# A graph layer's 8192 x 8192 adjacency product, streamed in loads of 8 MB through two ring slots instead of 4.5 MB through four

## The chip, the core and the metric

The kernel runs on one core of a Trainium2 chip. The metric is the device time of one execution in microseconds (us). The kernel before took 643.39 us, the median of 3 runs (643.38 to 643.44).

## What is computed

```python
agg = adj @ (x @ W_agg)                       # adj 8192 x 8192, x 8192 x 64, float32
y   = w[:, None] * relu(agg) + (1.0 - w)[:, None] * x
out = layernorm(x + y)                        # over the 64 columns of a row, eps 1e-5
```

`adj` is nearly all zeros but is given dense, 268.4 MB in float32.

## The kernel before

The host hands `adj` over transposed and cut into blocks, so that every load is contiguous in DRAM; this is not in the metric. The 64 row tiles of 128 rows are done in groups: `G` = 6 main groups of nine (`MAIN_SLOTS`), one mid group of nine (`MID_SLOTS`), and one last row tile. For a group the contraction runs over 64 k-tiles of 128. A main load (L128, L132) brings eight k-tiles (`SUB`) for nine row tiles: 128 partitions with one row of 8 x 9 x 128 x 4 = 36,864 bytes each, 4608 KB. `C` = 8 loads make a group. They go round a ring of four slots (`RING`). SP issues all of them on one DMA queue. Before each it waits on `slot_free`, which PE raises when it has used up the load that was in that slot (L127, L131, L135).

PE computes the transposed aggregate with `x` as the stationary operand (`contract`, L182 to L190). The array's 128 columns are used as two halves of 64. The halves take k-tiles of even and odd number, so the two halves of a bank hold partial sums, in three banks of 384 columns. `turn_back` (L192 to L201) then multiplies by `W_agg`, stacked twice in `wagg2`, which turns the sum round to rows and adds the halves. Before it ACT copies the banks to `aggT` (L257). Every product in the code is two records in the trace: 8 x 3 x 2 = 48 in all for a load, of 384 columns each. DVE does relu, residual and normalisation (L304 to L314, L292 to L302) beside the next group's loads.

The mid group is loaded in the same way, its last two loads in pieces of 4, 4 and 2, 2, 2, 2 k-tiles (`MID_TAIL`, L139 to L144), so that PE is soon done after the last. Then SP issues the store of the first 54 row tiles (L146), waits for slot 0 (L148), and issues ten loads of the last row tile into it (L150 to L153, `LAST_LOADS`). PE works these off (L222 to L229), the last two k-tiles against a ready `x @ W_agg` (L233 to L235), and the last rows are normalised and stored from ACT's queue (L269). The mid rows' store follows on SP's queue (L156).

Of the kernel before, what the change touches and what calls it, by code (L numbers as in the profile page):

```python
# [17 lines left out]
def gnn_residual_layernorm(nc, x, adj_main, adj_mid, adj_last, w, w_agg, out):  # L18
# [21 lines left out]
    BANKS = 3  # L40
    CHUNK = COLS // BANKS
    PER_BANK = MAIN_SLOTS // BANKS
# [4 lines left out]
    assert DIRECT_J0 % 2 == 0 and all(sum(pieces) == SUB for pieces in MID_TAIL) and MID_SLOTS == MAIN_SLOTS  # L47
# [11 lines left out]
    with ctx:  # L59
# [8 lines left out]

        ring = sb("ring", [P, RING, SUB * COLS])
        x_sb = sb("x_sb", [P, T, D])  # L70
# [5 lines left out]
        wagg2 = sb("wagg2", [P, D])  # L76
        ident = sb("ident", [P, P])
        eps = sb("eps", [P, 1])
        aggT = sb("aggT", [P, COLS])
# [13 lines left out]
        acc = bank[:, 0:BANKS]  # L93
        last_acc = bank[:, 3]
        last_rows = bank[:, 4, 0:D]

        xT_ps = bank[:, 3, 0:PAIRS * P]
        xw_ps = [bank[:, 4 + h, 0:PAIRS * D].rearrange("p (n d) -> p n d", d=D) for h in range(2)]
        rows_ps = bank[:, 5:5 + BANKS, 0:PER_BANK * D]

# [4 lines left out]
        x_in, w_in, wagg_in = sem("x_in"), sem("w_in"), sem("wagg_in")  # L105
        ident_zero, ident_ready = sem("ident_zero"), sem("ident_ready")
# [3 lines left out]
        last_done = sem("last_done")  # L110
# [9 lines left out]
        @block.sync  # L120
        def _(sp):
            sp.dma_start(x_sb[:], x.rearrange("(p t) d -> p t d", p=P)).then_inc(x_in, 16)  # L122
            sp.dma_start(w_sb[:], w.rearrange("(p t) -> p t", p=P)).then_inc(w_in, 16)  # L123
            for c in range(C):
                if c >= RING:

                    sp.wait_ge(slot_free, c - RING + 1)  # L127
                sp.dma_start(ring[:, c % RING], adj_main[0, c].rearrange("q s n -> q (s n)")).then_inc(loaded[c % RING], 16)  # L128
            with sp.Fori(1, G) as g:
                for c in range(C):  # L130
                    sp.wait_ge(slot_free, g * C + (c - RING + 1))  # L131
                    sp.dma_start(ring[:, c % RING],  # L132
                                 adj_main[bass.ds(g, 1), c].rearrange("o q s n -> (o q) (s n)")).then_inc(loaded[c % RING], 16)
            for c in range(C):
                sp.wait_ge(slot_free, MID * C + c - RING + 1)  # L135
                if c < WHOLE:
                    sp.dma_start(ring[:, c % RING], adj_mid[c].rearrange("q s n -> q (s n)")).then_inc(loaded[c % RING], 16)
                else:
                    s = 0  # L139
                    for k, n in enumerate(MID_TAIL[c - WHOLE]):  # L140
                        sp.dma_start(ring[:, c % RING, s * COLS:(s + n) * COLS],
                                     adj_mid[c, :, s:s + n].rearrange("q s n -> q (s n)")
                                     ).then_inc(mid_tail_loaded[c - WHOLE][k], 16)
# [12 lines left out]
            sp.dma_start(out_rows[:, MID_T0:LAST_T0], res[:, MID_T0:LAST_T0]).then_inc(stored, 16)  # L156

        @block.gpsimd
        def _(pool):
            nc.gpsimd.memset(ident[:], 0.0).then_inc(ident_zero, 1)  # L160
            pool.wait_ge(ident_zero, 1)
            nc.gpsimd.affine_select(out=ident[:], in_=ident[:], compare_op=ALU.not_equal, fill=1.0, base=0,
                                    pattern=[[-1, P]], channel_multiplier=1).then_inc(ident_ready, 1)
            nc.gpsimd.memset(eps[:], EPS).then_inc(eps_ready, 1)

        @block.tensor
        def _(pe):
# [14 lines left out]
            def contract(slot, j0, s0, n):  # L182
                for s in range(s0, s0 + n, 2):
                    for b in range(BANKS):
                        for h in range(2):
                            j = j0 + s + h
                            at = (s + h) * COLS + b * CHUNK
                            last = nc.tensor.matmul(acc[h * D:(h + 1) * D, b, 0:CHUNK], x_sb[:, j], ring[:, slot, at:at + CHUNK],  # L188
                                                    start=j < 2, stop=j >= T - 2)
                return last  # L190

            def turn_back(g):  # L192

                pe.wait_ge(dve_step, g * DVE_GROUP + DVE_PRE)
                for b in range(BANKS):
                    pe.wait_ge(agg_copied, g * BANKS + (b + 1))
                    for i in range(PER_BANK):
                        at = (b * PER_BANK + i) * P
                        last = nc.tensor.matmul(rows_ps[:, b, i * D:(i + 1) * D], aggT[:, at:at + P], wagg2[:],  # L199
                                                start=True, stop=True)  # L200
                    last.then_inc(rows_done, 1)  # L201

            with pe.Fori(0, G) as g:
                for c in range(C):
                    pe.wait_ge(loaded[c % RING], g * (16 * C // RING) + arrivals(c))
                    contract(c % RING, c * SUB, 0, SUB).then_inc(slot_free, 1)
                turn_back(g)
            for c in range(WHOLE):
                pe.wait_ge(loaded[c % RING], arrivals(MID * C + c))
                contract(c % RING, c * SUB, 0, SUB).then_inc(slot_free, 1)  # L210
            for i, pieces in enumerate(MID_TAIL):
                c = WHOLE + i
                s = 0
                for k, n in enumerate(pieces):
                    pe.wait_ge(mid_tail_loaded[i][k], 16)
                    last = contract(c % RING, c * SUB, s, n)
                    s += n
                last.then_inc(slot_free, 1)

            j = 0  # L220
            turn_back(MID)
            for k, n in enumerate(LAST_LOADS[:-1]):  # L222
                pe.wait_ge(last_loaded[k], 16)
                for s in range(n):
                    h = (j + s) % 2
                    last = nc.tensor.matmul(last_acc[h * D:(h + 1) * D, 0:P], x_sb[:, j + s],  # L226
                                            ring[:, 0, (j + s) * P:(j + s + 1) * P],
                                            start=j + s < 2, stop=j + s >= DIRECT_J0 - 2)
                j += n  # L229
# [3 lines left out]
            for j in range(DIRECT_J0, T):  # L233
                nc.tensor.matmul(last_rows, ring[:, 0, j * P:(j + 1) * P], xw[:, (j - DIRECT_J0) // 2, (j - DIRECT_J0) % 2],  # L234
                                 start=j == DIRECT_J0, stop=False)  # L235

            pe.wait_ge(agg_copied, LAST * BANKS + 1)
# [3 lines left out]
        def _(act):  # L241
            for h in range(2):
                act.dma_start(wagg2[h * D:(h + 1) * D, :], w_agg).then_inc(wagg_in, 16)

# [9 lines left out]
            def group(g):  # L254
                act.wait_ge(slot_free, g * C + C)
                for b in range(BANKS):
                    nc.scalar.copy(aggT[:, b * CHUNK:(b + 1) * CHUNK], acc[:, b, 0:CHUNK]).then_inc(agg_copied, 1)  # L257
                std_of(std[:], varsum[:], 1.0 / D, g * DVE_GROUP + (DVE_PRE + VAR_STEP))

            with act.Fori(0, G) as g:  # L260
                group(g)

                act.wait_ge(out_ready, g + 1)
            group(MID)
# [9 lines left out]
        def _(dve):  # L274
# [29 lines left out]
            with dve.Fori(0, LAST) as g:  # L304
                base = g * DVE_GROUP + DVE_PRE
                for b in range(BANKS):
                    dve.wait_ge(rows_done, g * BANKS + (b + 1))
                    slots = bass.ds(g * MAIN_SLOTS + b * PER_BANK, PER_BANK)
                    last = nc.vector.scalar_tensor_tensor(out=y[:, b * PER_BANK:(b + 1) * PER_BANK],  # L309
                                                          in0=rows_ps[:, b].rearrange("p (n d) -> p n d", d=D),  # L310
                                                          scalar=0.0, in1=over_row(w_sb[:, slots]),
                                                          op0=ALU.max, op1=ALU.mult)
                step(last, base + 1)
                normalise(g, g * MAIN_SLOTS, MAIN_SLOTS, base)  # L314

            v, t = y_last[:], LAST_T0
            dve.wait_ge(rows_done, LAST * BANKS + 1)
# [40 lines left out]
```

## Time and profile before

| | us |
|---|---|
| median of 3 runs | 643.39 |
| the profiled execution, its own time | 643.17 |
| span of its instructions | 641.1 |
| PE busy (matmuls) | 509.9 (80%) |
| DVE busy | 47.1 (7%) |
| ACT busy | 12.9 (2%) |
| DMA queue q1, share of 16 engines | 99.1% |
| read from HBM / written | 270.60 MB / 2.10 MB |

The profile is of one execution on the chip. Outside the span lie 643.17 - 641.1 = 2.1 us. Engine names: PE is the matrix engine, PEld its weight loads, DVE and ACT the vector and scalar engines, SPq and ACTq the instruction queues that issue DMAs. A packet is one row of one partition, or the 4 bytes with which a DMA engine reports its part of a load; a packet is placed by its start.

### The profile page before, as it was taken

To read this page: it belongs to the slowest core of one execution; us is meant where nothing else is said; L and a number is where in the kernel's file an instruction comes from. 1 tells how busy PE (TensorE), PEld (TensorE's weight loads), DVE (VectorE), ACT (ScalarE), POOL (GpSimd) and SP (SyncE) were. 2 spreads that over 40 slices of the span, in tenths; PEclk is the share of its full clock that TensorE was granted. 3 is DMA by queue.
4 is the path that set the end of the run, shared out by engine and by line. 5 is a ranking of instruction groups with operands and counts; after the bars stand their busy time and mean duration, and the time that the engine had idled before them with its cause. 6 is when DMAs were issued, how large, how long until landed. Compare 5 with 4: busy or idle time off the path is not lost.

```text
span 641.1 us, 6455 instructions
## 1 busy us (share of the span) xinstructions
PE 509.9 (80%) x2949; PEld 222.1 (35%) x2949; DVE 47.1 (7%) x80; ACT 12.9 (2%) x32; POOL 0.7 (0%) x7
## 2 busy tenths in 40 slices
PE   0778888878697878797788888796979788878896
PEld 0233334323233323242333343232424234333335
DVE  3000002000003000030000030000300000300004
ACT  0000000000000000000000000000000000000000
POOL 0000000000000000000000000000000000000000
PEclk9989889889999988998898898999998889898999
DMA  9999999999999999999999999999999999999996
GB/s 363 435 440 437 415 435 440 435 416 437 442 432 419 437 439 435 414 442 439 430 419 442 439 428 421 442 439 423 426 442 437 426 426 442 436 423 427 424 421 261
DMA packets 10967, 272.81 MB, mean 426 GB/s; under 512 B 1616, under 2 KB 2000, under 8 KB 3024
## 3 DMA queue, kind: packets, MB, share of 16 engines
q1 hardware_dynamic: 10656, 272.63, 99.1%
q8 instruction: 7, 0.11, 0.1%
q10 hardware_dynamic: 304, 0.07, 0.0%
HBM read 270.60 MB, written 2.10 MB: 425 GB/s over the span
## 4 chain that ended last, share of the span: by engine, by line
DMA 77%; PE 20%; SPq 2%; issue 0%; DVE 0%; ACT 0%; DVEq 0%
DMA ring<-adj_main_dram 62%; PE bank L188 19%; DMA ring<-adj_mid_dram 11%; DMA ring<-adj_last_dram 4%; SPq L151 1%; PE bank L226 1%; PE bank L199 0%; SPq L128 0%; SPq L132 0%; PE bank L234 0%; ACT aggT L257 0%; SPq L123 0%; SPq L122 0%; DVE res L324 0%; ACT std_last L252 0%
## 5 line engine op out<-in xcount | busy, mean ns | idle before, releaser
L188 PE MATMUL bank<-ring,x_sb 128*64 128x384 f32 x2688 | 484.6, 521 | 112.2 <-DMA ring<-adj_main_dram 99.8
L188 PEld LDWEIGHTS bank<-ring,x_sb 128*64 128x64 f32 x2688 | 199.2, 146 | 393.8 <-issue 248.2
L309 DVE SCALAR_TENSOR_TENSOR y<-bank,w_sb 128x192 f32<-128x192 f32 x21 | 7.5, 358 | 571.7 <-PE bank L199 571.7
L257 ACT COPY aggT<-bank 128x384 f32<-128x384 f32 x21 | 8.7, 487 | 568.4 <-PE bank L188 568.4
L199 PE MATMUL bank<-wagg,aggT 128*128 128x64 f32 x126 | 15.5, 277 | 4.1 <-ACT aggT L257 4.1
L199 PEld LDWEIGHTS bank<-wagg,aggT 128*128 128x128 f32 x126 | 14.6, 192 | 8.8 <-ACT aggT L257 7.5
L226 PE MATMUL bank<-ring,x_sb 128*64 128x128 f32 x124 | 7.9, 278 | 1.6 <-DMA ring<-adj_last_dram 1.5
L226 PEld LDWEIGHTS bank<-ring,x_sb 128*64 128x64 f32 x124 | 6.8, 136 | 2.6 <-DMA ring<-adj_last_dram 2.4
L172 PE MATMUL bank<-ident,x_sb 128*128 128x128 f32 x1 | 0.4, 447 | 8.9 <-DMA x_sb<-x_dram 8.9
L294 DVE TENSOR_TENSOR y<-y,res 128x576 f32<-128x576 f32 x7 | 5.3, 758 | 1.0
L296 DVE SCALAR_TENSOR_TENSOR y<-rowsum,y 128x576 f32<-128x576 f32 x7 | 5.3, 759 | 0.2
L302 DVE TENSOR_TENSOR res<-y,rstd 128x576 f32 x7 | 5.3, 758 | 0.2
L298 DVE TENSOR_TENSOR sq<-y 128x576 f32<-128x576 f32 x7 | 5.3, 757 | 0.2
L299 DVE TENSOR_REDUCE varsum<-sq 128x9 f32<-128x576 f32 x7 | 5.3, 754 | 0.2
L295 DVE TENSOR_REDUCE rowsum<-y 128x9 f32<-128x576 f32 x7 | 5.3, 754 | 0.2
L290 DVE TENSOR_TENSOR res<-x_sb,two_minus_w 128x4096 f32<-128x4096 f32 x1 | 4.4, 4427 | 0.0
L172 PEld LDWEIGHTS bank<-ident,x_sb 128*128 128x128 f32 x1 | 0.2, 183 | 8.8 <-issue 8.8
L252 ACT ACTIVATE std<-varsum,eps 128x9 f32<-128x9 f32 x7 | 2.1, 303 | 42.9 <-DVE varsum L299 42.9
L301 DVE RECIPROCAL rstd<-std 128x9 f32<-128x9 f32 x7 | 1.5, 216 | 2.6 <-ACT std L252 2.6
L245 ACT ACT_TABLE_LOAD x1 | 1.3, 1283 | 2.0 <-issue 2.0
L284 DVE COPY xw<-bank 128x64 f32<-128x64 f32 x2 | 0.4, 220 | 10.5 <-PE bank L178 10.5
L178 PE MATMUL bank<-wagg,xT 64*128 64x64 f32 x4 | 0.7, 437 | 0.4 <-ACT xT L247 0.4
(22 smaller groups left out, 5.8 us busy)
## 6 DMA issues: line engine op xcount, KB each, us to landing
ring<-adj_main_dram SPq DMA_DIRECT2D x48, 4608.0 KB, 35.5
ring<-adj_mid_dram SPq DMA_DIRECT2D x6, 4608.0 KB, 34.8
ring<-adj_mid_dram SPq DMA_DIRECT2D x2, 2304.0 KB, 32.8
ring<-adj_mid_dram SPq DMA_DIRECT2D x4, 1152.0 KB, 29.5
x_sb<-x_dram SPq DMA_DIRECT2D x1, 2048.0 KB, 8.0
out_dram<-res SPq DMA_DIRECT2D x1, 1728.0 KB, 36.7
ring<-adj_last_dram SPq DMA_DIRECT2D x2, 768.0 KB, 32.5
ring<-adj_last_dram SPq DMA_DIRECT2D x1, 640.0 KB, 26.2
```

The lines of the kernel that those rows point to most:

```text
L151: sp.dma_start(ring[:, 0, j * P:(j + n) * P], adj_last[:, j:j + n].rearrange("q s n -> q (s n)")).then_inc(last_loaded[k], 16)
L188: last = nc.tensor.matmul(acc[h * D:(h + 1) * D, b, 0:CHUNK], x_sb[:, j], ring[:, slot, at:at + CHUNK], start=j < 2, stop=j >= T - 2)
L199: last = nc.tensor.matmul(rows_ps[:, b, i * D:(i + 1) * D], aggT[:, at:at + P], wagg2[:], start=True, stop=True)
L226: last = nc.tensor.matmul(last_acc[h * D:(h + 1) * D, 0:P], x_sb[:, j + s], ring[:, 0, (j + s) * P:(j + s + 1) * P], start=j + s < 2, stop ...
L257: nc.scalar.copy(aggT[:, b * CHUNK:(b + 1) * CHUNK], acc[:, b, 0:CHUNK]).then_inc(agg_copied, 1)
L294: step(nc.vector.tensor_tensor(v, v, residual, ALU.add), base + 2)
L295: step(nc.vector.tensor_reduce(rowsum[:, 0:n], v, AX.X, ALU.add), base + 3)
L296: step(nc.vector.scalar_tensor_tensor(out=v, in0=over_row(rowsum[:, 0:n]), scalar=-1.0 / D, in1=v, op0=ALU.mult, op1=ALU.add), base + 4)
L298: step(nc.vector.tensor_tensor(s, v, v, ALU.mult), base + 5)
L299: step(nc.vector.tensor_reduce(varsum[:, 0:n], s, AX.X, ALU.add), base + VAR_STEP)
L302: nc.vector.tensor_tensor(residual, v, over_row(rstd[:, 0:n]), ALU.mult).then_inc(out_ready, 1)
L309: last = nc.vector.scalar_tensor_tensor(out=y[:, b * PER_BANK:(b + 1) * PER_BANK], in0=rows_ps[:, b].rearrange("p (n d) -> p n d", d=D), s ...
```

## The change

A load becomes sixteen k-tiles for eight row tiles: rows of 65,536 bytes, 8192 KB, four loads to a group. There are seven main groups of eight, a mid group of seven and the last row tile. The ring has two slots. The last row tile's loads have a buffer of their own (`last_sb`), and no wait before them. In a main group the column halves of the array take row tiles 0 to 3 and 4 to 7, with the same k-tile: one bank of 512 columns, two products (four records) to a k-tile, 64 records to a load. Turning back takes four products with a block diagonal `wagg_diag` (zeroed by POOL, filled by two DMAs on ACT's queue). The mid group keeps the halves by k-tile, in two banks of 448 columns; its rows are 57,344 bytes, its last two loads are cut into 8, 8 and 4, 4, 4, 2, 2. ACT makes one copy per group, DVE's relu step is two instructions in a main group and one in the mid group. Cut to its core:

```diff
-MAIN_SLOTS = 9
-MID_SLOTS = 9
+MAIN_SLOTS = 8
+MID_SLOTS = 7
-SUB = 8
-RING = 4
-MID_TAIL = ((4, 4), (2, 2, 2, 2))
+SUB = 16
+RING = 2
+MID_TAIL = ((8, 8), (4, 4, 4, 2, 2))
+        last_sb = sb("last_sb", [P, T * P])
+        wagg_diag = sb("wagg_diag", [P, P])
...
             sp.dma_start(out_rows[:, 0:MID_T0], res[:, 0:MID_T0]).then_inc(stored, 16)
-
-            sp.wait_ge(slot_free, LAST * C - RING + 1)
             j = 0
             for k, n in enumerate(LAST_LOADS):
-                sp.dma_start(ring[:, 0, j * P:(j + n) * P],
+                sp.dma_start(last_sb[:, j * P:(j + n) * P],
...
+            nc.gpsimd.memset(wagg_diag[:], 0.0).then_inc(diag_zero, 1)
...
+            def main_loads(g):
                 for c in range(C):
                     pe.wait_ge(loaded[c % RING], g * (16 * C // RING) + arrivals(c))
-                    contract(c % RING, c * SUB, 0, SUB).then_inc(slot_free, 1)
+                    for s in range(SUB):
+                        j = c * SUB + s
+                        for h in range(2):
+                            at = s * COLS + h * HALF * P
+                            last = nc.tensor.matmul(acc[h * D:(h + 1) * D, :], x_sb[:, j], ring[:, c % RING, at:at + HALF * P],
+                                                    start=j == 0, stop=j == T - 1)
+                    last.then_inc(slot_free, 1)
+
+            def turn_back(g):
+                pe.wait_ge(agg_copied, g + 1)
+
+                pe.wait_ge(dve_step, g * DVE_GROUP + DVE_PRE)
+                for k in range(HALF):
+                    last = nc.tensor.matmul(rows_ps[:, k * P:(k + 1) * P], aggT[:, k * P:(k + 1) * P], wagg_diag[:],
+                                            start=True, stop=True)
+                last.then_inc(rows_done, 1)
+
+            pe.wait_ge(diag_in, 32)
+            with pe.Fori(0, G) as g:
+                main_loads(g)
                 turn_back(g)
...
+            last.then_inc(mid_done, 1)
+            pe.wait_ge(agg_copied, G + 1)
+            for i in range(MID_SLOTS):
+                turned = nc.tensor.matmul(mid_rows[:, i * D:(i + 1) * D], aggT[:, i * P:(i + 1) * P], wagg2[:],
+                                          start=True, stop=True)
+            turned.then_inc(rows_done, 1)
...
+            act.wait_ge(diag_zero, 1)
+            for h in range(2):
+                act.dma_start(wagg_diag[h * D:(h + 1) * D, h * D:(h + 1) * D], w_agg).then_inc(diag_in, 16)
...
+                nc.scalar.copy(aggT[:, 0:HALF * P], acc).then_inc(agg_copied, 1)
...
+            nc.scalar.copy(aggT[:].rearrange("p (b n) -> p b n", b=MID_BANKS), mid_acc).then_inc(agg_copied, 1)
```

## Rows read from the trace of the kernel before

**Rows 1.** The page, 40 slices of 16 us: DMA engines' busy tenths, and GB/s.
```profile
DMA  9999999999999999999999999999999999999996
GB/s 363 435 440 437 415 435 440 435 416 437 442 432 419 437 439 435 414 442 439 430 419 442 439 428 421 442 439 423 426 442 437 426 426 442 436 423 427 424 421 261
```

**Rows 2.** The page, chain of work that ended last, by engine and by line.
```profile
DMA 77%; PE 20%; SPq 2%; issue 0%; DVE 0%; ACT 0%; DVEq 0%
DMA ring<-adj_main_dram 62%; PE bank L188 19%; DMA ring<-adj_mid_dram 11%; DMA ring<-adj_last_dram 4%; SPq L151 1%; PE bank L226 1%; PE bank L199 0%; SPq L128 0%; SPq L132 0%; PE bank L234 0%; ACT aggT L257 0%; SPq L123 0%; SPq L122 0%; DVE res L324 0%; ACT std_last L252 0%
```

**Rows 3.** Costliest groups: busy us, mean ns of one, idle before and its releaser.
```profile
L188 PE MATMUL bank<-ring,x_sb 128*64 128x384 f32 x2688 | 484.6, 521 | 112.2 <-DMA ring<-adj_main_dram 99.8
L296 DVE SCALAR_TENSOR_TENSOR y<-rowsum,y 128x576 f32<-128x576 f32 x7 | 5.3, 759 | 0.2
```

**Rows 4.** Issues on SP's queue: KB each, median us from issue to landing.
```profile
ring<-adj_main_dram SPq DMA_DIRECT2D x48, 4608.0 KB, 35.5
```

**Rows 5.** DMA of 97.45:446.83, 32 main loads: packets, then queue q1 (packets, MB, share).
```profile
DMA packets 4608, 150.98 MB, mean 432 GB/s; under 512 B 512, under 2 KB 512, under 8 KB 512
q1 hardware_dynamic: 4607, 150.96, 100.3%
```

**Rows 6.** DMA of 602:633: mid pieces, the store, the last row tile's loads.
```profile
DMA packets 1827, 12.96 MB, mean 418 GB/s; under 512 B 204, under 2 KB 238, under 8 KB 1031
```

**Rows 7.** By stretch: length, busy PE, PEld, DVE, ACT, POOL, granted clock, DMA share, GB/s.
```profile
152.04:160.00 7.96, 7.96 (x48) 3.36 (x48) 0.00 (x0) 0.00 (x0) 0.00 (x0) 1.00 1.03 445
173.85:183.50 9.65, 9.63 (x48) 3.90 (x48) 0.00 (x0) 0.00 (x0) 0.00 (x0) 0.82 0.99 428
315.80:325.97 10.17, 10.17 (x46) 4.16 (x48) 0.00 (x0) 0.00 (x0) 0.00 (x0) 0.71 1.03 442
```

**Rows 8.** The chain in order of time, its longest piece of PE: start, us, what.
```profile
315.80 10.90 PE bank L188 x48
```

**Rows 9.** PE in order of time: start, us, records, [idle before and its releaser].
```profile
97.45 2.80 PE L188 MATMUL bank<-ring,x_sb 128*64 128x384 f32 x16 [1.45 <-DMA ring<-adj_main_dram]
162.95 7.96 PE L188 MATMUL bank<-ring,x_sb 128*64 128x384 f32 x48 [2.95 <-DMA ring<-adj_main_dram]
173.87 9.65 PE L188 MATMUL bank<-ring,x_sb 128*64 128x384 f32 x48 [2.96 <-DMA ring<-adj_main_dram]
195.71 7.96 PE L188 MATMUL bank<-ring,x_sb 128*64 128x384 f32 x48 [0.16 <-DMA ring<-adj_main_dram]
630.96 5.33 PE L226 MATMUL bank<-ring,x_sb 128*64 128x128 f32 x84 [0.35 <-DMA ring<-adj_last_dram]
```

**Rows 10.** Packets of 96.75:97.00, then of 97.00:97.25, before the load used from 97.45.
```profile
DMA packets 5, 0.11 MB, mean 442 GB/s; under 512 B 2, under 2 KB 2, under 8 KB 2
DMA packets 1, 0.04 MB, mean 147 GB/s; under 512 B 0, under 2 KB 0, under 8 KB 0
```

**Rows 11.** The last store: its issue, and GB/s of 638.5:641.1 in 40 slices.
```profile
639.14 0.35 ACTq L269 DMA_DIRECT2D out_dram<-res  x1
GB/s 0 0 0 0 0 0 0 0 0 0 0 0 0 0 0 0 0 0 0 0 0 0 0 110 225 134 36 0 0 0 0 0 0 0 0 0 0 0 0 0
```

**Rows 12.** Around a group's end: start, us, what, [idle before].
```profile
105.45 1.24 ACT L257 COPY aggT<-bank 128x384 f32<-128x384 f32 x3 [95.84 <-PE bank L188]
105.98 2.22 PE L199 MATMUL bank<-wagg,aggT 128*128 128x64 f32 x18 [0.58 <-ACT aggT L257]
```

**Rows 13.** PE at the end of the mid group and in the last row tile.
```profile
621.80 2.16 PE L188 MATMUL bank<-ring,x_sb 128*64 128x384 f32 x12 [0.59 <-DMA ring<-adj_mid_dram]
624.62 2.19 PE L199 MATMUL bank<-wagg,aggT 128*128 128x64 f32 x18 [0.67 <-ACT aggT L257]
627.20 1.09 PE L226 MATMUL bank<-ring,x_sb 128*64 128x128 f32 x16 [0.38 <-DMA ring<-adj_last_dram]
632.54 3.50 PEld L226 LDWEIGHTS bank<-ring,x_sb 128*64 128x64 f32 x60 [0.30 <-DMA ring<-adj_last_dram]
```

More of the change, by code:

```diff
@@ L46, in gnn_residual_layernorm @@
     assert C * SUB == T == sum(LAST_LOADS) and LAST_T0 + LAST_SLOTS == T and C % RING == 0
-    assert DIRECT_J0 % 2 == 0 and all(sum(pieces) == SUB for pieces in MID_TAIL) and MID_SLOTS == MAIN_SLOTS
+    assert DIRECT_J0 % 2 == 0 and all(sum(pieces) == SUB for pieces in MID_TAIL) and HALF * P == 512
     DVE_PRE = 2
@@ L92, in gnn_residual_layernorm @@
         bank = psum("bank", [P, 8, 512])
-        acc = bank[:, 0:BANKS]
+        acc = bank[:, 0]
+        mid_acc = bank[:, 1:1 + MID_BANKS, 0:MID_CHUNK]
         last_acc = bank[:, 3]
         last_rows = bank[:, 4, 0:D]
+        rows_ps = bank[:, 5]
+        mid_rows = bank[:, 6, 0:MID_SLOTS * D]
         xT_ps = bank[:, 3, 0:PAIRS * P]
-        xw_ps = [bank[:, 4 + h, 0:PAIRS * D].rearrange("p (n d) -> p n d", d=D) for h in range(2)]
-        rows_ps = bank[:, 5:5 + BANKS, 0:PER_BANK * D]
+        xw_ps = [bank[:, 6 + h, 0:PAIRS * D].rearrange("p (n d) -> p n d", d=D) for h in range(2)]
         loaded = [sem(f"loaded{r}") for r in range(RING)]
@@ L180, in _ @@
             last.then_inc(xw_done, 1)
[L182 to L201, printed above, removed]
@@ new lines, in mid_contract @@
+            def mid_contract(c, s0, n):
+                for s in range(s0, s0 + n, 2):
+                    for b in range(MID_BANKS):
+                        for h in range(2):
+                            j = c * SUB + s + h
+                            at = (s + h) * MID_COLS + b * MID_CHUNK
+                            last = nc.tensor.matmul(mid_acc[h * D:(h + 1) * D, b], x_sb[:, j],
+                                                    ring[:, c % RING, at:at + MID_CHUNK], start=j < 2, stop=j >= T - 2)
+                return last
@@ L215, in _ @@
                     pe.wait_ge(mid_tail_loaded[i][k], 16)
-                    last = contract(c % RING, c * SUB, s, n)
+                    last = mid_contract(WHOLE + i, s, n)
                     s += n
-                last.then_inc(slot_free, 1)
+            last.then_inc(mid_done, 1)
[4 more added lines that the diff above has]
+            turned.then_inc(rows_done, 1)
             j = 0
-            turn_back(MID)
             for k, n in enumerate(LAST_LOADS[:-1]):
@@ L243, in _ @@
                 act.dma_start(wagg2[h * D:(h + 1) * D, :], w_agg).then_inc(wagg_in, 16)
+            act.wait_ge(diag_zero, 1)
+            for h in range(2):
+                act.dma_start(wagg_diag[h * D:(h + 1) * D, h * D:(h + 1) * D], w_agg).then_inc(diag_in, 16)
             nc.scalar.preload_act_table_set("sqrt_and_others")
@@ L252, in std_of @@
                 nc.scalar.activation(out_std, var, ACT.Sqrt, bias=eps[:, 0:1], scale=scale).then_inc(std_ready, 1)
-            def group(g):
+            with act.Fori(0, G) as g:
                 act.wait_ge(slot_free, g * C + C)
-                for b in range(BANKS):
-                    nc.scalar.copy(aggT[:, b * CHUNK:(b + 1) * CHUNK], acc[:, b, 0:CHUNK]).then_inc(agg_copied, 1)
+                nc.scalar.copy(aggT[:, 0:HALF * P], acc).then_inc(agg_copied, 1)
                 std_of(std[:], varsum[:], 1.0 / D, g * DVE_GROUP + (DVE_PRE + VAR_STEP))
-            with act.Fori(0, G) as g:
-                group(g)
                 act.wait_ge(out_ready, g + 1)
-            group(MID)
+            act.wait_ge(mid_done, 1)
+            nc.scalar.copy(aggT[:].rearrange("p (b n) -> p b n", b=MID_BANKS), mid_acc).then_inc(agg_copied, 1)
+            std_of(std[:, 0:MID_SLOTS], varsum[:, 0:MID_SLOTS], 1.0 / D, MID * DVE_GROUP + DVE_PRE + VAR_STEP)
             act.wait_ge(last_done, 1)
@@ L302, in normalise @@
                 nc.vector.tensor_tensor(residual, v, over_row(rstd[:, 0:n]), ALU.mult).then_inc(out_ready, 1)
-            with dve.Fori(0, LAST) as g:
+            with dve.Fori(0, G) as g:
                 base = g * DVE_GROUP + DVE_PRE
[L306 to L312, printed above, removed]
+                dve.wait_ge(rows_done, g + 1)
+                for h in range(2):
+                    last = nc.vector.scalar_tensor_tensor(
+                        out=y[:, h * HALF:(h + 1) * HALF],
+                        in0=rows_ps.rearrange("p (k h d) -> p h k d", h=2, d=D)[:, h], scalar=0.0,
+                        in1=over_row(w_sb[:, bass.ds(g * MAIN_SLOTS + h * HALF, HALF)]), op0=ALU.max, op1=ALU.mult)
                 step(last, base + 1)
                 normalise(g, g * MAIN_SLOTS, MAIN_SLOTS, base)
+            base = MID * DVE_GROUP + DVE_PRE
+            dve.wait_ge(rows_done, G + 1)
+            step(nc.vector.scalar_tensor_tensor(out=y[:, 0:MID_SLOTS], in0=mid_rows.rearrange("p (n d) -> p n d", d=D),
+                                                scalar=0.0, in1=over_row(w_sb[:, MID_T0:LAST_T0]),
+                                                op0=ALU.max, op1=ALU.mult), base + 1)
+            normalise(MID, MID_T0, MID_SLOTS, base)
             v, t = y_last[:], LAST_T0
-            dve.wait_ge(rows_done, LAST * BANKS + 1)
+            dve.wait_ge(rows_done, LAST + 1)
             step(nc.vector.tensor_scalar(v, last_rows, 0.0, w_sb[:, t:t + 1], ALU.max, ALU.mult), LAST_STEP0 + 1)
```

30 lines of the change are left out of this document (15 added, 15 removed).

## Prediction

> **What bounds the kernel now.** I read the slices first. The DMA engines are at nine tenths or more in every slice but the last, at 414 to 442 GB/s, save the first, which holds the start [rows 1]. The chain of waits says the same: 77% of it is DMA, and the 20% that it gives to PE are PE working on a load while the queue behind it is full [rows 2]. PE waits for loads 112 us in all [rows 3]. A main load takes 35.5 us from issue to landing though its data need a quarter of that: 32 loads took 349.38 us, 10.92 us each [rows 4, 5]. So some three loads always stand in the queue, and the q1 share is 100.3% [rows 5]. Nothing that PE, ACT or DVE save counts; only bytes, packets, or a queue that runs dry can move the time.
>
> **Price of a packet.** Two stretches with full engines but different rows. In the first (349.38 us, 16 engines: 5590 engine-us) 4608 packets carry 150.98 MB; in the second (31 us, 496 engine-us) 1827 packets carry 12.96 MB [rows 5, 6]. With a time per byte and a time per packet, two equations give 27.26 GB/s per engine and 11.3 ns per packet. The second stretch's MB are rounded, and it holds stores as well; 0.04 MB is 1.5 us of engine time, so I take 10 ns, with 5 and 13 as bounds. Below it could be nothing, if the lower rate of the second stretch (418 against 432 GB/s) is not the packets' doing.
>
> **Packets saved.** Per engine a load is 8 rows and one report, 9 packets. Before: 54 whole loads and 6 pieces, 60 x 9 = 540. After: 7 x 4 = 28 main, 2 whole mid loads and 7 pieces, 37 x 9 = 333. Saved: 207 x 10 ns = 2.1 us (1.0 to 2.7). The last row tile's ten loads are as before, as are the bytes of `adj`, `x` and the output.
> The Trainium skill (DMA: Bandwidth & Descriptors, section Why small descriptors are slow) puts a packet's fixed cost at about 3 cycles, and the section Where 436 GB/s comes from puts the cycle at 850 MHz: by that estimate 3.5 ns, and the saving 0.7 us, 642.7 us in all. The two stretches disagree with it here by a factor of three.
>
> **Added.** Two small loads for `wagg_diag`, 4 rows of 256 bytes and a report on each engine, twice: 10 packets, about 0.15 us with their bytes, on full engines, so they count. POOL's extra memset and ACT's wait come before `x` has landed, and PE's wait for `diag_in` is long over when the first 8 MB land, at about 28 us. Sum: 2.1 - 0.15, some 1.9 us less.
>
> **Two slots.** This is the step that could cost. By the rates above a load now takes 8 x (2404 + 10) + 10 ns = 19.3 us. PE's records follow each other at 7.96 / 48 = 166 ns for 384 columns and 5.33 / 84 = 63 ns for 128 [rows 9]: 0.40 ns per column, so 217 ns for 512, or 221 in proportion. 64 records: 14.0 us. Before, a slot was refilled three loads ahead; now the refill is issued when PE is done, with one load left in the queue. Measured from the slowest engine's last byte of load c: PE starts 0.45 to 0.7 us later (last two reports in 96.75:97.00, PE at 97.45 [rows 9, 10]), works 14.0 us, SP issues, and the first packet starts 0.85 us after the issue (639.14, first bytes in the slice from 640.0 [rows 11]; nearest row, a small store, I take 0.9). That is 0.6 + 14.0 + 0.9 = 15.5 us against 19.3: 3.8 us to spare at the higher clock.
> The clock takes some of it. PE works at the granted clock 1.00 (2.4 GHz) in one load and at 0.82 or 0.71 in others, which mixes 2.4 and 1.2 GHz [rows 7]; of two loads before which PE had idled 2.95 and 2.96 us, one ran at the higher level throughout and one did not [rows 7, 9]. Idle time grows to 19.3 - 14.0 = 5.3 us, so I expect most loads to begin at 1.2 GHz. The worst load before took 10.90 instead of 7.96 us [rows 8, 9], 2.9 us more. If that is a stretch of fixed length: 14.0 + 2.9 = 16.9, and 18.4 us with the rest, 0.9 us to spare. If it grew with the load (14.0 x 10.90 / 7.96 = 19.2 us) the queue would run dry by 1.4 us. I take the first, since the higher clock returned inside each load, and since a longer busy time shortens the next idle one. I cost the two slots at nothing; the cover is the 0.9 us.
>
> **Turning back.** Before: 0.5 us of copy, 2.2 us for 18 records, and PE is still back in time, with 0.16 us idle [rows 9, 12]. After: one copy of 512 columns, about 0.6 us, and 8 records of 128 columns at 123 to 170 ns, 1.4 us at most. After a slow last load PE is back at 16.9 + 2.0 = 18.9 us, before the next load; and `slot_free` has been raised before it, so the refill does not wait for it. DVE's work is seven or eight instructions of under 0.76 us [rows 3], beside a group of 77 us; ACT's is one copy. Neither is waited for.
>
> **The end.** The store before the last loads grows by 2 row tiles and the mid store shrinks by 2. The queue order is the same. Before, PE took up the last mid piece at 621.80, and the first last load reached it at 627.20, 5.4 us later, after 0.38 us idle [rows 13]. After: 2 k-tiles x 4 records x 193 ns = 1.5 us, one copy of 896 columns (0.9 us), 14 records (1.7 us): 4.2 us, still hidden. From 632.54 PE's pace sets the end, 60 records and the last products [rows 13]: unchanged. The wait for slot 0 that goes was hidden by a full queue. So the DMA saving passes through whole.
>
> **Sum.** 643.17 - 1.9 = 641.2 for a profiled execution, whose span would be 639.2; its own time stood 0.2 below the median, so the median comes out at 641.5 us. A measurement of this kernel can tell about 0.2%, 1.3 us, from no change.
>
> **Rivals.**
> 1. No gain: a 64 KB row is moved as two packets, or the packet price is far under 10 ns. Split rows make 28 x 17 + 2 x 9 + 63 = 557 packets against 540: with `wagg_diag` 0.3 us more, 643.7. Nothing in the trace moved more than 36,864 bytes in one packet, so the profile can't exclude it. A price of 3 or 4 ns gives 642.7. Chance 0.17, at 643.5.
> 2. Slower, the queue runs dry. It decides at a PE time of 19.3 - 0.6 - 0.9 = 17.8 us per load; beyond it each us costs a us on each load. Where the low clock lasts in proportion, 1.4 us on each of the 30 whole loads is 42 us; on every third load it is 14 us: 643.4 - 1.9 + 14 = 655.5. For it: idle grows from 2.96 to 5.3 us, and the start of a transfer is known only from a small store. Against it: the worst load of 56 had 2.9 us of loss. Chance 0.17.
> 3. Slower, the rate itself falls. In the new layout the partitions' rows lie 65,536 bytes apart in DRAM, and engines in step read at large powers of two from each other; before it was 36,864. The last loads already have a power of two, 32,768, and their stretch ran at 418 instead of 432 GB/s [rows 5, 6]. If that was the pitch and not the packets, the 235 MB of main loads at 418 take 18 us more: 661.6. Against it: the packet price explains the whole difference, and the pieces of the mid group in that stretch have no such pitch. Chance 0.06.
> The Trainium skill (DMA: Bandwidth & Descriptors, Latency and other measured facts) reports copies with rows 512 KiB apart at 207 GB/s, against 214 at full rate, and 103 at 4 MiB; by 3% it would be some 20 us here. No run yet shows a pitch of 64 KiB on this chip.
>
> **How the numbers follow.** The forecast, 641.5 us, has 0.60; its own range is 640.6 to 642.6 by the packet's bounds, and 0.04 of it lies within 0.2% of the time before (above 642.1). So faster 0.56, no change 0.04 + 0.17 = 0.21, slower 0.17 + 0.06 = 0.23. The range takes the forecast, the first rival and the mild end of the second (the queue dry by 0.3 us on ten loads): 640.3 to 646.0. What it leaves out is the larger part of rivals 2 and 3, under 0.2.
>
> **What would show it.** Right: in a stretch of whole main groups, 9 packets per engine per load, 433.5 GB/s or a little above, q1 share 100%; main loads landing every 19.3 us; issue to landing about 22 us (19.3 plus what is left of the load before it); PE idle 2 to 5 us before each, with low clock at many starts. Wrong: twice as many data packets (rival 1); SP's refills issued later than 17.8 us after a landing and a q1 share under 100% (rival 2); full engines at fewer GB/s (rival 3).

## The result and the profile after

The changed kernel takes 662.08 us (median of 4, 658.65 to 664.19) against 643.41 us beside it: 1.0285 of the time before, 95% interval 1.0266 to 1.0304. It is slower by 18.7 us where 1.9 us less was forecast. The profiled execution took 658.65 us with a span of 656.9.

The page after, DMA engines' busy tenths and GB/s in 40 slices of 16 us, to be held against [rows 1], and the chain of work that ended last, against [rows 2]:

```profile
DMA  9999999899999999999999999999999999999995
GB/s 389 447 383 436 443 388 431 371 423 447 443 387 447 383 439 447 391 435 395 447 447 443 427 407 447 439 391 447 443 427 379 411 447 447 399 416 422 394 395 213
...
q1 hardware_dynamic: 7344, 272.63, 97.7%
...
DMA 59%; PE 37%; SPq 3%; issue 0%; DVE 0%; ACT 0%; DVEq 0%
```

The bytes are the same, the packets fewer, and yet slices of 371 to 395 GB/s now stand between slices of 447. PE's share of the chain has gone from 20% to 37%: PE is what releases a load's slot, and the DMA queue now waits for that. q1's share of the engines has fallen from 99.1% to 97.7%. Even that understates it, as the next views show.

PE in order of time (start, us, records, idle before and its releaser), against [rows 9]; the starts are the landings of the loads:

```profile
28.39 16.68 PE L194 MATMUL bank<-ring,x_sb 128*64 128x512 f32 x64 [17.80 <-DMA ring<-adj_main_dram]
47.73 15.55 PE L194 MATMUL bank<-ring,x_sb 128*64 128x512 f32 x64 [2.66 <-DMA ring<-adj_main_dram]
69.28 16.72 PE L194 MATMUL bank<-ring,x_sb 128*64 128x512 f32 x64 [6.00 <-DMA ring<-adj_main_dram]
88.92 15.44 PE L194 MATMUL bank<-ring,x_sb 128*64 128x512 f32 x64 [2.93 <-DMA ring<-adj_main_dram]
...
208.76 16.95 PE L194 MATMUL bank<-ring,x_sb 128*64 128x512 f32 x64 [5.69 <-DMA ring<-adj_main_dram]
...
288.91 16.13 PE L194 MATMUL bank<-ring,x_sb 128*64 128x512 f32 x64 [5.67 <-DMA ring<-adj_main_dram]
308.25 13.95 PE L194 MATMUL bank<-ring,x_sb 128*64 128x512 f32 x64 [3.21 <-DMA ring<-adj_main_dram]
```

From 288.91 to 308.25 is 19.34 us, the forecast's length of a load; from 47.73 to 69.28 it is 21.55. From the second landing (47.73) to the last main one (563.02) there are 26 loads in 515.3 us; at 19.35 each they take 503.1. So 12.2 us are lost in the main groups. PE takes 13.95 us for a load at the full granted clock, and up to 16.95 where the clock is lower:

```profile
208.76:225.71 16.95, 16.95 (x64) 5.08 (x64) 0.00 (x0) 0.00 (x0) 0.00 (x0) 0.82 1.00 433
269.28:283.23 13.95, 13.95 (x64) 4.51 (x64) 4.65 (x8) 0.30 (x1) 0.00 (x0) 1.00 0.93 404
```

(By stretch, columns as in [rows 7].) Both lengths are the forecast's own, 14.0 and 16.9. What was not forecast is what happens in the queue. This is the refill of the slot that PE, at work from 28.39 on, has used up: its issue, then the packets of three stretches, those under 512 bytes being the engines' reports on the load in front of it (such short stretches show more than the real rate, since a packet counts whole where it starts):

```profile
45.11 0.33 SPq L133 DMA_DIRECT2D ring<-adj_main_dram  x1
```

```profile
DMA packets 27, 0.72 MB, mean 901 GB/s; under 512 B 16, under 2 KB 16, under 8 KB 16
DMA packets 3, 0.20 MB, mean 246 GB/s; under 512 B 0, under 2 KB 0, under 8 KB 0
DMA packets 2, 0.13 MB, mean 218 GB/s; under 512 B 0, under 2 KB 0, under 8 KB 0
```

They are 46.4:47.2, 47.2:48.0 and 48.4:49.0. All 16 engines have reported by 47.2, but only 11 have begun the new load by then, three more by 48.0, and the last two after 48.4, at 48.6 and 48.8, 3.5 and 3.6 us after the issue. These first rows took 2.5 to 3.4 us in the trace, where a row takes 2.42 us otherwise. An engine that has run empty starts late and slowly.

The plainest case is in run e8 below, where all 16 engines had been empty for 4.8 us when the refill was issued. The issue, and the packets of 52.88:54.8:

```profile
52.88 0.33 SPq L133 DMA_DIRECT2D ring<-adj_main_dram  x1
DMA packets 16, 1.05 MB, mean 546 GB/s; under 512 B 0, under 2 KB 0, under 8 KB 0
```

The first of the 16 rows starts at 53.84, 0.97 us after the issue, the last at 54.71, 1.8 us after it, and they take 2.8 to 3.3 us each.

I call the time from a refill's issue to the first engine's report on the load in front of it the lead: how much the engine that is furthest ahead still had to do. Of the 26 main refills after the second landing, read one by one in the trace, with the excess of the landing interval over 19.35 us:

| lead | refills | excess in all |
|---|---|---|
| under 2 us (four of them negative: issued after the first engine was empty) | 10 | 9.2 us |
| 2.0 to 2.9 us | 7 | 2.5 us |
| 3.1 us and over | 9 | 0.5 us |

The table goes by the first engine, while a load has landed only with the last, so it is no law for the single refill: the load behind a lead of -0.5 us (issue 127.13) took 19.3 us, because the engines that ran empty were those that were ahead; their reports came 2.7 us apart before it and 0.6 us after it.

Not all of this loss comes from the leads. In e2 below, where leads are 7.3 us and over, one interval is still 1.3 us too long (20.6 us, landing at 87.3). In it one packet of 16 KB passes on the queue that the page calls "instruction" (from 71.27, for 1.1 us). The row that starts right behind it, at 72.35, takes 2.89 us, and one engine is late from then on: the reports on a load come 1.8 us apart instead of 0.5. The queues of e2 in 70:76:

```profile
q1 hardware_dynamic: 37, 2.42, 93.8%
q8 instruction: 1, 0.02, 1.1%
```

The kernel before has such packets too; with one of them, at 36.6, its load that lands at 42.2 takes 12.0 us instead of 10.9. In the changed kernel two of them, at 52.53 and 92.78, fall into two of the four longest intervals, which the trace can't divide between the two causes.

The rest of the loss is in the mid group, whose loads are shorter still (16.9 us) and are issued behind PE's work on an 8-tile load (leads of 0.4 and 0.9 us for the second and the fourth). From the last main landing (563.02) to the last mid piece it takes 73.4 us; in e2 below, where PE is out of the way, it takes 68.2.

```profile
636.43 1.72 PE L218 MATMUL bank<-ring,x_sb 128*64 128x448 f32 x8 [0.51 <-DMA ring<-adj_mid_dram]
```

### The profile page after: what moved, and what is told of

It reads as the page before. It is cut to its first block, busy times and chain, and to the rows that moved or that the text cites. A ratio compares the mean times of both kernels' runs of the same rounds, so it can differ in the third digit from the quotient of the medians.

```text
span 656.9 us, 4963 instructions
## 1 busy us (share of the span) xinstructions
PE 506.4 (77%) x2253; PEld 171.2 (26%) x2253; DVE 46.5 (7%) x81; ACT 9.5 (1%) x20; POOL 0.9 (0%) x8
## 3 DMA queue, kind: packets, MB, share of 16 engines
q1 hardware_dynamic: 7344, 272.63, 97.7%
## 4 chain that ended last, share of the span: by engine, by line
DMA 59%; PE 37%; SPq 3%; issue 0%; DVE 0%; ACT 0%; DVEq 0%
DMA ring<-adj_main_dram 53%; PE bank L194 34%; DMA last_sb<-adj_last_dram 3%; DMA ring<-adj_mid_dram 3%; PE bank L218 2%; SPq L155 2%; SPq L147 0%; SPq L137 0%; PE bank L251 0%; SPq L152 0%; PE bank L243 0%; SPq L128 0%; SPq L133 0%; SPq L127 0%; DVE res L348 0%
## 5 line engine op out<-in xcount | busy, mean ns | idle before, releaser
L194 PE MATMUL bank<-ring,x_sb 128*64 128x512 f32 x1792 | 434.0, 646 | 122.5 <-DMA ring<-adj_main_dram 122.5
L194 PEld LDWEIGHTS bank<-ring,x_sb 128*64 128x64 f32 x1792 | 134.8, 149 | 416.9 <-issue 274.6
L218 PE MATMUL bank<-ring,x_sb 128*64 128x448 f32 x256 | 51.5, 564 | 6.2 <-DMA ring<-adj_mid_dram 6.2
L218 PEld LDWEIGHTS bank<-ring,x_sb 128*64 128x64 f32 x256 | 18.6, 143 | 38.4 <-issue 30.6
L203 PE MATMUL bank<-wagg_diag,aggT 128*128 128x128 f32 x56 | 8.1, 287 | 5.4 <-ACT aggT L276 5.4
L243 PE MATMUL bank<-last_sb,x_sb 128*64 128x128 f32 x124 | 9.2, 308 | 2.0 <-DMA last_sb<-adj_last_dram 2.0
L203 PEld LDWEIGHTS bank<-wagg_diag,aggT 128*128 128x128 f32 x56 | 6.8, 191 | 11.5 <-issue 11.5
L243 PEld LDWEIGHTS bank<-last_sb,x_sb 128*64 128x64 f32 x124 | 8.0, 156 | 3.1 <-DMA last_sb<-adj_last_dram 3.0
L312 DVE TENSOR_TENSOR y<-y,res 128x512 f32<-128x512 f32 (+1 forms) x8 | 5.5, 684 | 1.0
L314 DVE SCALAR_TENSOR_TENSOR y<-rowsum,y 128x512 f32<-128x512 f32 (+1 forms) x8 | 5.5, 684 | 0.3
L234 PE MATMUL bank<-wagg,aggT 128*128 128x64 f32 x14 | 1.8, 278 | 1.0 <-ACT aggT L281 1.0
## 6 DMA issues: line engine op xcount, KB each, us to landing
ring<-adj_mid_dram SPq DMA_DIRECT2D x2, 3584.0 KB, 19.3
```

The costliest lines, as they stand in the source:

```text
L194: last = nc.tensor.matmul(acc[h * D:(h + 1) * D, :], x_sb[:, j], ring[:, c % RING, at:at + HALF * P], start=j == 0, stop=j == T - 1)
L203: last = nc.tensor.matmul(rows_ps[:, k * P:(k + 1) * P], aggT[:, k * P:(k + 1) * P], wagg_diag[:], start=True, stop=True)
L218: last = nc.tensor.matmul(mid_acc[h * D:(h + 1) * D, b], x_sb[:, j], ring[:, c % RING, at:at + MID_CHUNK], start=j < 2, stop=j >= T - 2)
L312: step(nc.vector.tensor_tensor(v, v, residual, ALU.add), base + 2)
L314: step(nc.vector.scalar_tensor_tensor(out=v, in0=over_row(rowsum[:, 0:n]), scalar=-1.0 / D, in1=v, op0=ALU.mult, op1=ALU.add), base + 4)
```

## The experiments

Theory 1: two slots leave the queue too short a lead, since an engine that has run empty starts 1 to 4 us after the issue. Theory 2: rows of 64 KB, a power of two apart, are read more slowly. Theory 3: PE's new work, with the halves by row tile, is what is slow.

**e1, four slots of half the size**

```diff
-SUB = 16
-RING = 2
-MID_TAIL = ((8, 8), (4, 4, 4, 2, 2))
+SUB = 8
+RING = 4
+MID_TAIL = ((4, 4), (2, 2, 2, 2))
```

> The changed kernel with eight k-tiles to a load and four slots: rows of 32,768 bytes, the ring's bytes, the halves by row tile and everything else as changed. Theory 1 (the queue runs dry: with two slots a refill is issued 0 to 4 us before the first engine is through, and an engine that ran empty starts 1 to 4 us after the issue and slowly): three loads stand in the queue, no loss; 37 + 32 whole loads and pieces less, 612 packets per engine instead of 540 at 10 ns, so about 644 us, and 431 to 432 GB/s in the main loads. Theory 2 (rows whose distance is a power of two are read slower): 32,768 is one as well, 655 us or more with full engines. Theory 3 (the halves by row tile make PE slower or wake it later): stays at 655 to 662.

Measured: 644.32 us, ratio 1.0018 (1.0008 to 1.0027). All but a microsecond of the loss is gone with the ring's bytes, the halves and the row tiles unchanged, and the rows still a power of two apart (32,768). Theory 3 falls; theory 2 is left only for 65,536 itself.

**e2, half of PE's products**

```diff
-                    for s in range(SUB):
+                    for s in range(0, SUB, 2):
...
-                for s in range(s0, s0 + n, 2):
+                for s in range(s0, s0 + n, 4):
```

> The changed kernel, loads untouched, but PE uses only every second k-tile of a main load and every second pair of a mid load (half of the contraction is left out). PE needs about 7 to 9 us per load, so a refill is issued 8 us or more before the queue would run dry. Theory 1: 641.0 to 641.8 us, 433 GB/s, loads landing every 19.35 us: the forecast's packet saving at last. Theory 2 (the rate of 64 KB rows): stays near 660. Theory 3: no statement on PE, but with PE out of the way also 641.

Measured: 642.27 us, ratio 0.9979 (0.9968 to 0.9991). The queue with its 64 KB rows runs at full rate. PE in order of time, and the packets of 184.56:532.86, 18 loads:

```profile
184.56 8.49 PE L194 MATMUL bank<-ring,x_sb 128*64 128x512 f32 x32 [7.81 <-DMA ring<-adj_main_dram]
203.91 9.05 PE L194 MATMUL bank<-ring,x_sb 128*64 128x512 f32 x32 [10.87 <-DMA ring<-adj_main_dram]
223.26 9.61 PE L194 MATMUL bank<-ring,x_sb 128*64 128x512 f32 x32 [10.31 <-DMA ring<-adj_main_dram]
...
620.44 1.72 PE L218 MATMUL bank<-ring,x_sb 128*64 128x448 f32 x8 [0.43 <-DMA ring<-adj_mid_dram]
```

```profile
DMA packets 2592, 151.00 MB, mean 434 GB/s; under 512 B 288, under 2 KB 288, under 8 KB 288
```

19.35 us from landing to landing, 434 GB/s against 432 before [rows 5], and 2592 packets for 18 loads are 9 per engine and load: a 64 KB row is one packet. Theory 2 falls, and so does the first rival of the prediction. This is what the forecast described, with PE's pace taken away.

**e3 and e5, PE kept busy between the loads**

```diff
+            def keep_busy(n):
+                for i in range(n):
+                    h = i % 2
+                    nc.tensor.matmul(bank[h * D:(h + 1) * D, 7, :], x_sb[:, 0],
+                                     x_sb[:, 0:HALF * P // D].rearrange("p t d -> p (t d)"), start=True, stop=True)
...
                     last.then_inc(slot_free, 1)
+                    if c < C - 1:
+                        keep_busy(8)
...
                 turn_back(g)
+                keep_busy(4)
...
                 mid_contract(c, 0, SUB).then_inc(slot_free, 1)
+                keep_busy(6)
```

This is e5; e3 has `h = 0` throughout, and 3 products after a turning back.

> The changed kernel with idle products added on PE after each load has been released (8 after a main load, 3 after a turning back, 6 after a mid load, into a bank nobody reads), so that PE's idle gaps stay under about 2 us. Theory 1 with the clock as its cause: nearly all main loads take 13.95 us instead of 15.5 to 16.9, refills go out some 4.4 us before the first engine is through, and the time falls to 641.5 to 644 us. If the clock isn't the cause, or a lead of 4.4 us is not enough, it stays at 655 to 662. Theory 2: no change, 660.

Measured: 667.77 us, ratio 1.0374 (1.0357 to 1.0392), slower still. PE in order of time:

```profile
125.28 6.60 PE L189 MATMUL bank<-x_sb 128*64 128x512 f32 x15
131.72 0.59 PE L189 MATMUL bank<-x_sb 128*64 128x512 f32 x1
131.78 14.27 PE L199 MATMUL bank<-ring,x_sb 128*64 128x512 f32 x63
145.88 6.60 PE L189 MATMUL bank<-x_sb 128*64 128x512 f32 x15
```

The idle products took 6.6 us instead of 3.5, so a load cost PE 20.6 us (125.28 to 145.88), more than the 19.35 of its transfer. They all wrote the same column half: 16 records, the first started at 125.28 and the last at 131.72, 429 ns from one to the next (the 413 ns of the next expectation divide by 16 where 15 steps belong). PE itself was the bound, so the run says nothing on the theories. The next one alternates the halves:

> As e3, but the idle products alternate between the two column halves, as the real ones do. In e3 they all wrote one half and took 413 ns a record instead of 217, so PE worked 20.6 us per load of 19.35 and was itself the bound; here 8 products are 16 x 217 ns = 3.5 us, in all 17.5 us per load. Theory 1, with the clock as the cause of the short leads: main loads at 13.95 us throughout, refills 3.9 to 4.5 us before the first engine is through, 641.3 to 643 us and q1 at 99%. If the leads are long and the time stays at 655 or more, theory 1 falls.

Measured: 651.04 us, ratio 1.0126 (1.0099 to 1.0154); the profiled execution, 654.87 us, is one of the slower ones. More than half of the loss is gone, but not all, and 641.3 to 643 was missed. The clock still fell in many loads, after gaps of 2.0 to 3.4 us:

```profile
149.12 13.95 PE L200 MATMUL bank<-ring,x_sb 128*64 128x512 f32 x64 [1.70 <-DMA ring<-adj_main_dram]
168.47 13.95 PE L200 MATMUL bank<-ring,x_sb 128*64 128x512 f32 x64 [1.96 <-DMA ring<-adj_main_dram]
...
326.02 15.65 PE L200 MATMUL bank<-ring,x_sb 128*64 128x512 f32 x64 [3.36 <-DMA ring<-adj_main_dram]
```

**e4, the kernel before with two slots**

```diff
-RING = 4
+RING = 2
```

> The kernel before with two ring slots instead of four: same rows of 36,864 bytes, same PE work. PE takes 8.0 to 9.7 us of the 10.9 us of a load, so the refill goes out 0.5 to 2.3 us before the queue is dry. Theory 1: the same loss per refill as in the changed kernel but on twice as many refills: 0.5 to 1.5 us on each of some 60, 670 to 730 us, q1 share well under 100%. Theory 2: the row distance is as before, so 643.5, or 645 with the later start of the last loads.

Measured: 702.61 us, ratio 1.0915 (1.0865 to 1.0966), in the middle of the expected span, with rows, pitch and PE work of the kernel before. The DMA of 100:600:

```profile
DMA packets 6030, 197.50 MB, mean 395 GB/s; under 512 B 672, under 2 KB 672, under 8 KB 672
...
q1 hardware_dynamic: 6029, 197.48, 94.7%
```

**e7, the same with half of the products**

```diff
-RING = 4
-MID_TAIL = ((4, 4), (2, 2, 2, 2))
+RING = 2
+MID_TAIL = ((4, 4), (4, 4))
...
-                for s in range(s0, s0 + n, 2):
+                for s in range(s0, s0 + n, 4):
```

> The kernel before with two slots as in e4, and PE using only every second pair of k-tiles (half of the contraction is left out), last two mid loads in two pieces each. PE takes 4 to 5 us of a load's 10.9, so a refill goes out 5 us or more before the queue is dry. Theory 1 (the lead decides, not the number of slots): 643 to 646 us against e4's 702.6, the rest being the later start of the last loads. If two slots cost in themselves (one load in the queue is not enough to keep 16 engines going), 660 or more.

Measured: 653.59 us, ratio 1.0146 (1.0114 to 1.0177). 49 of e4's 59 us are gone, so it is the lead and not the number of slots that costs most; but 643 to 646 was missed. PE has little to do now and its mean granted clock is 0.765; half a load takes it mostly 5.4 to 7.1 us and not 4 to 5, and the leads are mostly 1 to 3.4 us, not 5:

```profile
576.26 5.51 PE L188 MATMUL bank<-ring,x_sb 128*64 128x384 f32 x24 [6.12 <-DMA ring<-adj_mid_dram]
587.26 6.83 PE L188 MATMUL bank<-ring,x_sb 128*64 128x384 f32 x24 [5.49 <-DMA ring<-adj_mid_dram]
```

**e9, seven eighths of the products**

```diff
-                    for s in range(SUB):
+                    for s in [k for k in range(SUB) if k not in (6, 7)]:
...
-                for s in range(s0, s0 + n, 2):
+                for s in [k for k in range(s0, s0 + n, 2) if k != 6]:
```

> The changed kernel with PE leaving out two of a load's sixteen k-tiles (an eighth of the contraction is left out), loads untouched. Every refill goes out some 1.8 to 2 us earlier than in the changed kernel, so that leads of 0 to 4.5 us become 2 to 6.5. Theory 1 with a needed lead of about 2.5 us: a few late refills are left, 642 to 646 us. If a refill had to be much earlier than that (5 us or more), little is won: 652 or more.

Measured: 646.39 us, ratio 1.0056 (1.0042 to 1.0069). Less than 2 us of PE's time per load brings back 15.7 of the 18.7 us. The leads in the main groups are 1.6 to 4.0 us here, and the main groups lose 1.7 us in all against 19.35 us per load.

**e8, e11, e10 and e12, the changed kernel with its leads restored**

e8 is e5 with more filling: 10 idle products after a main load, 6 after a turning back, 8 after a mid load, and 36 before the first load.

> As e5, with PE kept busy from before the first load (36 idle products) and with longer fill (10 after a main load, 6 after a turning back, 8 after a mid load), so that no idle gap is much over 1 us. In e5 the clock still fell in about half of the loads, after gaps of 1.96 us and more, and its refills then went out 0 to 2.2 us before the first engine was through. Theory 1: every main load 13.95 us, every lead over 3 us, loads every 19.35 us, 641.5 to 643.0 us. If PE's 18.3 us per load of 19.35 make the refills late after any disturbance, 645 to 650.

Measured: 653.05 us, ratio 1.0151 (1.0138 to 1.0164), outside the expectation. The trace shows why, and that the theory held where it applies:

```profile
38.93 13.90 PE L200 MATMUL bank<-ring,x_sb 128*64 128x512 f32 x64
56.96 13.90 PE L200 MATMUL bank<-ring,x_sb 128*64 128x512 f32 x64
75.88 13.95 PE L200 MATMUL bank<-ring,x_sb 128*64 128x512 f32 x64 [0.74 <-DMA ring<-adj_main_dram]
95.23 13.95 PE L200 MATMUL bank<-ring,x_sb 128*64 128x512 f32 x64 [1.10 <-DMA ring<-adj_main_dram]
...
559.68 13.95 PE L200 MATMUL bank<-ring,x_sb 128*64 128x512 f32 x64 [1.11 <-DMA ring<-adj_main_dram]
```

From 95.23 to 559.68, 24 loads take 464.45 us, 19.35 each: no loss at all with leads of 3.2 us. What is lost is lost before and behind: the 36 products held the first load back from 28.4 to 38.9, and the leads at the passage to the mid group are short again, 0.9 us for the second mid load and 0.0 us for the last.

e11 changes one number of e8, 36 to 14:

> e8 with 14 idle products before the first load instead of 36, nothing else; they end at about 28 us, when the first load lands. Theory 1: e8's loss at the start goes, 6 to 8 us, 645 to 647.5 us; the loss at the passage to the mid group stays. If the start had no part in it, 653.

Measured: 646.26 us, ratio 1.0039 (1.0028 to 1.0050), as expected. Its leads in the main groups are mostly 2.1 to 3.0 us and cost little: 3.7 us over 26 loads, 2.6 of them on the first two.

e10 adds to e11 a filling of the queue ahead of the mid group, `EARLY` = 3 loads of the last row tile (8, 12 and 12 k-tiles):

```diff
+            last_loads(0, EARLY)
             for c in range(C):
                 sp.wait_ge(slot_free, MID * C + c - RING + 1)
...
+            last_products(0, EARLY)
             for c in range(WHOLE):
                 pe.wait_ge(loaded[c % RING], arrivals(MID * C + c))
```

> As e11 (e8 with 14 idle products at the start instead of 36), and the first three loads of the last row tile (8, 12, 12 k-tiles, 2 MB, 4.9 us of the queue) go out before the mid group's, their products before the mid group's too. In e8 all main loads from the fourth on landed every 19.35 us, with leads of 3.2 us; it lost about 6 us at the start (PE took the first load up at 38.9 instead of 28.4, behind its idle products) and about 5 us at the passage to the mid group (leads 0.9 and 1.6). Theory 1: with both mended 641.3 to 643 us, at or below the kernel before. If a loss is left at the passage, 644 to 647.

Measured: 646.44 us, ratio 1.0043 (1.0030 to 1.0056): nothing won over e11, and 641.3 to 643 was missed. The reason that e12's expectation gives isn't in the profiled execution (651.03 us, the slowest of six): there PE took the first mid load up at 576.95, 0.5 us after its last report. Its short leads are 0.5 us at the first refill of the run and -0.6 us at the last mid load. The slot of that one was freed late: the second mid load, which was in it, landed only at 594.73 and took PE 13.9 us instead of 12.25.

e12 moves these products behind the first mid load and puts 8 idle products before the first load, 4 before the mid group and 6 after its second load:

> e10 with 8 idle products before the first load instead of 14 (in e10 they ended at 32.1 us, 3.7 us after the first load had landed), and the last row tile's first products moved behind the first mid load instead of before it (in e10 PE took that load up late, behind them, and the refill after it went out late). Theory 1: every lead 3 us or more from the first refill to the last piece, 641.5 to 643.5 us, at or below the kernel before. If leads are still short at one of the two places, 644 to 647.

Measured: 644.27 us, ratio 1.0014 (1.0005 to 1.0023). The mended kernel has won back 17.8 of the 18.7 us and comes within 0.9 us of the kernel before, not below it. In the profiled execution (643.54 us) all leads in the main groups are 3.0 us and over; two at the passage are 2.5 us (issues at 586.32 and 603.26). What also stands there is PE's own work:

```profile
605.63 24.22 PE L233 MATMUL bank<-ring,x_sb 128*64 128x448 f32 x128
```

It works without a pause until 629.85, 4.5 us after the last mid piece has landed (625.39). How much of the rest is PE's and how much the leads', no run separates.

**e6, the price of a packet**: the kernel before, each whole load as two DMAs of four k-tiles.

```diff
-                sp.dma_start(ring[:, c % RING], adj_main[0, c].rearrange("q s n -> q (s n)")).then_inc(loaded[c % RING], 16)
+                for k in range(2):
+                    sp.dma_start(ring[:, c % RING, k * 4 * COLS:(k + 1) * 4 * COLS],
+                                 adj_main[0, c, :, k * 4:(k + 1) * 4].rearrange("q s n -> q (s n)")).then_inc(loaded[c % RING], 16)
```

> The kernel before with each of its 54 whole loads issued as two DMAs of four k-tiles, rows of 18,432 instead of 36,864 bytes, nothing else. 54 x 9 = 486 more packets per engine. At the 10 ns of the forecast 4.9 us more, 648.2 us (2.4 more at 5 ns, 6.3 at 13 ns); by the Trainium skill's 3 cycles of the fabric (DMA: Bandwidth & Descriptors, Why small descriptors are slow) 1.7 us more, 645.1. If SP's issues or the queue's depth became the bound, the q1 share would fall under 99%.

Measured: 647.32 us, ratio 1.0063 (1.0050 to 1.0076): 3.9 us (3.2 to 4.9) for 486 packets per engine, 8.0 ns each (6.6 to 10.1). The 10 ns of the forecast is at the upper end; the 3.5 ns worked out from the Trainium skill (DMA: Bandwidth & Descriptors, section Why small descriptors are slow) is too low by about half.

## Why the prediction was wrong, step by step

- **What bounds the kernel**: right. In the kernel before only bytes, packets or a queue that runs dry can move the time, and the queue ran dry. (10.92 of 35.5 us is nearly a third, not a quarter; the three loads in the queue follow from that.)
- **Packets saved**: right in its mechanism, a little high in its size. 9 packets per engine and load, 8.0 ns instead of 10: 207 of them are 1.7 us. With PE out of the way (e2) the 1.9 us forecast was 1.0 us by the medians (0.6 to 2.1 by the interval of the ratio). The low end of the forecast's own range, 640.6, should read 640.9 by its terms (643.4 - 2.7 + 0.15).
- **Two slots**: this is the step that failed. PE's times, 14.0 and 16.9 us, were right, and so was the expectation that many loads would begin at the lower clock. The cost "I cost the two slots at nothing; the cover is the 0.9 us" was wrong: they cost some 17 us. Three things were wrong in the cover. It was reckoned to the slowest engine's last byte, while the engines report on a load 0.6 to 2.8 us apart, and the first of them runs dry that much earlier. It ended with the first packet, "0.85 us after the issue"; that figure held (0.97 us in e8's dry refill), but the last engine starts 1.8 us after the issue there and 3.6 us in the refill issued at 45.11. And the first rows then take up to 1.0 us longer than the others in that refill. So with PE at 16.95 us (208.76 to 225.71) the next refill, issued at 225.89, had not 0.9 us to spare but a lead of 0.5 us (first report 226.39), and that load took 2.3 us longer than 19.35. The condition was not a PE time under 17.8 us but a lead of 2 to 3 us: by the rows here 19.35 less 0.6 to 0.7 us from the last report to PE's start and from PE's end to the issue, less the spread, less PE's time, that is a PE time of 13 to 15 us for 3 us of lead, which only the full clock gives.
- **Sum**: 12.2 us in the main groups, 5.2 us at the mid group (73.4 against e2's 68.2), 0.5 us at the end (20.5 us from the last mid piece to the span's end, 20.0 in e2) make 17.9, against the 17.4 between the profiled execution and its forecast of 641.2. Of the 12.2, e2 has 1.3 too; without them it is 16.6, against the 16.5 between the spans of the changed kernel and e2 (656.9 - 640.4).
- **Rivals**: the second, with 0.17, named what happened, a queue that runs dry, but not when. Its condition, PE over 17.8 us, was never met (16.95 us at most), and its 655.5 us is made of loads of 19.2 us of which there was none; that it lies near the 662.08 is luck. The first fell by e2's packets and e6, the third by e2's 434 GB/s at a distance of 65,536 bytes.
- **Turning back and the end**: right in the main. PE came back in time (0.77 us of waiting for the copy, 1.15 us for 8 records). The end was forecast unchanged; from the last mid piece to the span's end it is 20.5 us against 19.3 before (641.1 - 621.80) and 20.0 in e2.

One thing stays open: why an empty engine starts late. The trace shows when the rows begin, not where the issue waits.

## What to carry to other kernels

A ring's depth is not its bytes: the same 128 KB per partition made 662 us as two slots and 644 us as four. Before giving up a slot, take the transfer time of a load, less the consumer's slowest time for one, less the spread of the engines, and ask for about 3 us of rest, and read that consumer's time at its lower clock, since longer waits between longer loads bring the clock down by themselves (0.937 on the mean before, 0.916 after). 3 us is on the safe side: in e9, e10 and e11, 54 main refills with leads of 2.0 to 2.9 us lost 2.6 us in all, but the changed kernel lost 2.5 us on seven of them. Larger rows had 1 to 2 us to give here; that is the first number to work out, and it was too small to risk the queue for.

## What the runs showed of the hardware

- An engine that runs empty costs more than the gap: the first rows of e8's dry refill took 2.8 to 3.3 us instead of 2.42. In e4 nearly every second load ran dry, and 59 us were lost on some 60 refills, with q1's share down to 94.7% only.
- One 16 KB packet on the queue "instruction" made one engine 1.3 us late for good (e2): with the queue full it cost one load 1.3 us and no other.
- Products that alternate between the two column halves of the array follow each other at 13.95 / 64 = 218 ns per record of 512 columns; products that stay in one half follow each other at 429 ns (e3). The same idle products, alternating, took 3.60 us for 16 records (e5). In the trace of e5 they start in pairs, 3 to 4 ns apart within a pair and 429 ns from pair to pair. The layouts of both kernels use that alternation.
- Idle products hold the clock: with gaps of 0.7 to 1.1 us (e8) it stayed at the full level through all main loads, with gaps of 2.0 to 3.4 us (e5) it fell in some loads and not in others.
